# A loop over 24 attention tiles, written out as a straight program, in a decoder layer with two attentions and a mixture of experts

## What is computed

```python
def layer(x, ctx, mask):                     # x (16, 256, 256), ctx (16, 77, 256), f32
    x = layernorm(x + attn(x))               # causal self-attention, 16 heads of 64, then projection
    x = layernorm(x + xattn(x, ctx, mask))   # attention over 77 context rows, 16 heads of 16
    x = layernorm(x + moe(x))                # 8 experts, top 2, capacity 1280, a fallback FFN, gelu
    return x
```

## Time and profile before

| | |
|---|---|
| median of 3 runs | 1939.02 us (1936.5 to 1940.05) |
| the profiled execution | 1935.39 us, its span 1933.6 us |
| granted clock of TensorE, mean over the span | 0.927 of full |
| TensorE busy | 1597.7 us, 21,330 matmuls |
| VectorE, ScalarE, GpSimd busy | 1258.6, 1036.6, 707.3 us |
| moved by DMA | 162.80 MB in 136,447 packets |

### The profile page before, as it was taken

The page is one execution under the profiler, slowest core; times in us unless marked ns, Lnnn a source line. Parts: engine busy times, 40 slices in busy tenths (PEclk is TensorE's granted clock), DMA queues, the critical chain, the costliest instruction groups (busy, mean ns, idle before and its releaser), DMA issues. The chain is left out here.

```text
span 1933.6 us, 59530 instructions
## 1 busy us (share of the span) xinstructions
PE 1597.7 (83%) x21330; PEld 1388.0 (72%) x21330; DVE 1258.6 (65%) x3008; ACT 1036.6 (54%) x2581; POOL 707.3 (37%) x910
## 2 busy tenths in 40 slices
PE   1999989898898988989889899985169999999920
PEld 1788878787787877878778788874068888888810
DVE  4577767676676766767667677764675555555556
ACT  4566666666666666666566666552004444444424
POOL 1134345453344534435343353342003334333311
PEclk9999999999999999999999999996559999999965
DMA  5342222223222232222233221100731111111145
GB/s 151 106 131 95 69 88 75 72 67 103 85 76 75 67 98 85 82 75 67 69 103 93 69 73 55 55 19 6 314 119 41 49 51 46 47 49 50 45 154 196
DMA packets 136447, 162.80 MB, mean 84 GB/s; under 512 B 78334, under 2 KB 110206, under 8 KB 133760
## 3 DMA queue, kind: packets, MB, share of 16 engines
q1 hardware_dynamic: 125056, 136.94, 21.5%
q0 software_dynamic: 6912, 17.84, 3.0%
q10 hardware_dynamic: 4224, 4.19, 0.6%
HBM read 93.92 MB, written 66.06 MB: 83 GB/s over the span
## 5 line engine op out<-in xcount | busy, mean ns | idle before, releaser
L1311 PE MATMUL ps_e<-xt,wres 128*128 128x128 f16 x3456 | 359.4, 220 | 0.2
L1311 PEld LDWEIGHTS ps_e<-xt,wres 128*128 x3456 | 292.1, 98 | 73.2 <-issue 0.6
L1360 ACT ACTIVATE act_g<-ps_e,b 128x128 f32<-128x128 f32 x576 | 164.3, 368 | 227.0 <-PE ps_e L1311 116.5
L1318 PE MATMUL ps_e<-wres,g_hi 128*128 x576 | 217.5, 379 | 1.1 <-DVE g_lo L1390 1.1
L881 POOL TENSOR_TENSOR o_st<-o_norm,o_st 128x256 f16<-128x256 f32 x128 | 85.9, 671 | 338.0 <-ACT o_st L602 337.9
L386 PE MATMUL ps<-x_hi,w_q 128*128 128x128 f16 x2048 | 197.2, 222 | 0.0
L590 ACT ACTIVATE probs<-ps,nbias 128x128 f32<-128x128 f32 (+1 forms) x512 | 187.3, 417 | 8.4
L386 PE MATMUL ps<-x_hi,w_k 128*128 128x128 f16 x2048 | 187.2, 219 | 0.0
L386 PE MATMUL ps<-x_lo,w_q 128*128 128x128 f16 x1024 | 181.9, 222 | 1.2 <-issue 1.2
L707 DVE TENSOR_REDUCE nmax<-ps 128x1 f32<-128x128 f32 (+1 forms) x512 | 157.5, 349 | 38.2 <-PE ps L401 34.3
L386 PE MATMUL ps<-x_lo,w_k 128*128 128x128 f16 x1024 | 176.5, 219 | 0.0
(11 more groups left out here) (257 smaller groups left out, 4830.2 us busy)
## 6 DMA issues: line engine op xcount, KB each, us to landing
piece<-in_moe_w SPq DMA_DIRECT2D x24, 768.0 KB, 6.5
w_scr<-piece_pair SPq DMA_DIRECT2D x24, 768.0 KB, 5.1
wres<-w_scr SPq DMA_DIRECT2D x18, 1024.0 KB, 22.3
v_scr<-v_tok SPq DMA_DIRECT2D x32, 512.0 KB, 2.7
v_pos<-v_scr SPq DMA_DIRECT2D x32, 512.0 KB, 4.5
z_scr<-zero SPq DMA_DIRECT2D x32, 256.0 KB, 3.7
f_z<-z_scr SPq DMA_DIRECT2D x8, 1024.0 KB, 5.7
x_t<-in_xT SPq DMA_DIRECT2D x32, 128.0 KB, 5.9
```

What stands on the lines that cost most here:

```text
L1311: last = mm(out, w(c * FF + f * P, b, P), xt[:, t % 2, a, c], start=(m == 0), stop=(m == 5))
L1318: mm(out[:, 0:2 * D], g_hi[:, t % G_BUFS, f], w(KC * FF + f * D, 0, 2 * D), start=(f == 0), stop=False, skip_group_check=True)
L1360: nc.scalar.activation(act_g[:, k % 2, f], ps[:, 3 + 2 * (k % 2) + f // 4, (f % 4) * P:(f % 4 + 1) * P], ACT.Gelu, bias=bias[:, f:f + 1], ...
```

## The change

The `Fori` of twelve turns with two steps each becomes a Python loop over 24 whole numbers, which writes every step out. `steps` no longer needs the engine. Nothing else is edited; with s a whole number the values of waits and the addresses are constants.

```diff
--- before.py
+++ after.py
@@ -258,7 +258,7 @@
 
     block = ctx.enter_context(nc.Block())
 
-    def steps(eng, step):
+    def steps(step):
 
 
         step(-1, 1, "NA")
@@ -266,9 +266,8 @@
         step(1, 1, "NABC")
         step(2, 0, "NABCD")
         step(3, 1, "NABCD")
-        with eng.Fori(2, BATCH - 2, 1) as b:
-            step(2 * b, 0, "NABCDW")
-            step(2 * b + 1, 1, "NABCDW")
+        for s in range(4, TILES - 4):
+            step(s, s % 2, "NABCDW")
         step(TILES - 4, 0, "NABCD")
         step(TILES - 3, 1, "NABCD")
         step(TILES - 2, 0, "ABCD")
@@ -353,7 +352,7 @@
                 sp.dma_start(weight_rows(io)[:, bass.ds(n * 2 * PIECE, 2 * PIECE)],
                              piece_pair[:].rearrange("p b k n -> p (b k n)")).then_inc(s_w_out, 16)
 
-        steps(sp, step)
+        steps(step)
         sp.wait_ge(s_z_out, 16 * (CODES // P) // 2)
         sp.wait_ge(s_w_out, 16 * (PIECES + 1))
         for p in range(2):
@@ -557,7 +556,7 @@
                 if "D" in stages and g >= 3:
                     stage_d(s - 2, p, g)
 
-        steps(pe, step)
+        steps(step)
 
 
     @block.scalar
@@ -676,7 +675,7 @@
                     act.wait_ge(s_w_hi, 2 * (s - 4) + 1)
                     nc.scalar.activation(piece[:], piece[:], ACT.Copy, scale=WP_UP).then_inc(s_w_hi, 1)
 
-        steps(act, step)
+        steps(step)
 
 
     @block.vector
@@ -851,7 +850,7 @@
         nc.vector.memset(v2_hi[:], 1.0).then_inc(s_one, 1)
         nc.vector.memset(sm[:], NEG2).then_inc(s_neg, 1)
         dve.wait_ge(s_neg, 1)
-        steps(dve, step)
+        steps(step)
 
 
     @block.gpsimd
@@ -952,7 +951,7 @@
                     nc.gpsimd.tensor_tensor(piece_pair[:, at, 1], piece[:].rearrange("p (b n) -> p b n", n=WBLOCK)[:, at], piece_pair[:, at, 0],
                                             ALU.subtract).then_inc(s_w_lo, 1)
 
-        steps(pool, step)
+        steps(step)
 
 
 def weight_rows(io):
```

## The result

The changed kernel takes 1874.74 us (1873.56 to 1876.16, four runs) against 1937.82 us before (four runs, the three of the table above and one more): ratio 0.9672, interval 0.9656 to 0.9687, 63.1 us or 3.3% faster. The profiled execution took 1876.16 us, its span is 1874.3 us against 1933.6.

A forecast was written before the change was run, and what follows sets the result against it. TensorE, 83% busy, was taken to bound the kernel, with idle gaps and a lower clock at each loop jump. 54.1 us for jumps plus 4.1 for registers, 58.2 off the 1939.02 median, gave 1880.8 us, range 1873 to 1890.

The forecast's parts named there:

- The jumps: Eleven jumps back of TensorE's loop: removing them was to save 54.1 us, idle time and slower matmuls together.
- Gaps: TensorE idle before L409, the body's first matmul, after each of eleven jumps: 35.7 us in all, to vanish.
- Lower clock: Even steps behind a jump run at 0.93 to 0.97 of full clock; 16.4 us to be saved.
- The register work: Sequencers computing wait values and addresses in the loop: 0 to 8.2 us to be saved, middle 4.1 taken.
- weight pieces: Extra ScalarE and GpSimd copies in the loop's steps, a possible other source of the 0.34 us a step.
- The instruction stream: Code fetch in the 24 steps: TensorE's packets from 130 to about 90, other engines' up 40 to 50; costed at nothing.
- Rival 1: Other engines' straight code arrives late, holding them about 3.25 us a packet: 2027 us, slower; chance 0.02.
- Rival 2: Weight pieces or x's load would end the loop's steps late anyway: at the limit no change, 1939; chance 0.02.
- next late thing: In straight steps, TensorE's waits before L493 and L526, about 3 us a step, were to remain the bound.
- Rival 3: Late TensorE packets or lower clock in the straight 24 steps, losing 1 us a step: 1905; chance 0.06.
- Rival 4: Python steps with whole numbers would emit other code than with a register; chance 0.01 at most.
- The sum: Whole kernel: 54.1 + 4.1 = 58.2 us saved, ends 54.1 and 62.3, giving 1880.8 us; chance 0.90.

The follow-up runs named there:

- the announced jump: The kernel before, loop and registers kept, with a hint on TensorE's loop announcing its jump back; 1884.81 us, ratio 0.9726.
- the shorter body: The kernel before with its loop, each projection taking only the first of its three products, TensorE's body 1,595 records instead of 2,139; 1869.26 us, with less work.
- the code sizes: The changed kernel plus a block behind its end: every engine loops over bodies of some 100 to 2,200 satisfied waits, in two runs; the block's time means nothing.
- the jump to held code: The changed kernel with, on TensorE alone, a two-turn loop of one semaphore increment behind each odd step, 12 jumps back; 1875.17 us.
- the registers' run: The changed kernel's 24 written-out steps, but each pair takes its tile number from a register, without a jump; 1883.39 us, ratio 0.9715.

## Why the prediction was right, and where it was off

**The jumps.** Predicted 54.1 us, from the two undisturbed loop steps of the earlier trace rows. The runs confirm both parts and the way they hang together. Gaps: 35.7 us gone. Cause: the fetch of a target that is not held (the announced jump, the shorter body, the code sizes, and against them the jump to held code). Lower clock: TensorE's busy time in the steps went from 868.65 to 844.15 us. Not all of these 24.5 us are time of the kernel. The fair comparison is the registers' run, which has the same register work and no jumps. There TensorE is busy 844.86 us, 23.8 less than in the loop before, and idle 72.5 us, where the loop before, without its gaps, has 66.8. TensorE, late behind each jump, thus waited 5.7 us less for others, 5.0 of it for VectorE's o_norm. 35.7 us of gaps and 23.8 of slower work less these 5.7 are the 53.8 by which the two differ. The prediction took the step lengths (16.4 us) and not the busy time (22.0), and so had this right without naming it; its sentence that the 16.4 shows as busy time leaves 5.6 us open. The loop without its jumps is 917.3 us as predicted (917.0 from 12 x (37.67 + 38.75)).

**The register work.** This is the term that was mis-sized. The prediction bounded it by 0 and 8.2 us, put it down to registers or weight pieces, and took the middle, 4.1. It measured 8.0 (917.32 - 909.28), and the weight pieces cost nothing. VectorE carries about 0.1 us a step and TensorE most of the rest. So the upper end was true. Both reasons that the prediction gave, that register work sits in the chains between engines and that the copies of the pieces fall into ScalarE's idle time, pointed there, and the middle was taken against them.

**The instruction stream.** About 90 packets were predicted for TensorE's 24 steps, 98 came; 40 to 50 for the others, 37 came in place of 4. None held an engine: the 24 step lengths agree to 0.02 us. Rival 1 is out, though its price was real. A fetch that is not ahead cost the other engines 2.4 to 3.3 us in the table above; straight code is brought ahead, a far jump is not.

**Rival 2** (the gap as a cover) is out as it was put, since L492 and L525 wait no longer than they did. In small there was a cover: the wait for o_norm, 5.7 us before and 12.0 after. The prediction's next late thing was mis-sized too: the waits before L493 and L526 are 1.6 us a step ((31.4 + 6.7) / 24), and the 3 us are all of TensorE's idle time in a step. **Rival 3** (late packets) did not occur in straight code; late packets did occur, in small, in the loop with the announced jump. **Rival 4** is out, since the order and count of matmuls are the same.

**The sum.** Predicted 58.2, with ends of 54.1 and 62.3. In the steps it is 61.9, of which 54 for jumps and 8 for registers; between the medians 63.1, with 1.2 us of scatter outside the steps in it. The measured 1874.74 lies 6.1 us under the 1880.8 forecast and near the low end of the range: 3.7 us by the steps, nearly all of it the register term, 1.2 by that scatter, and 1.2 because the fourth run of the kernel before took its median from 1939.02 to 1937.82, which is luck of the runs. The Trainium skill, "Advanced Engine Details and Errata", section Control Flow Timing, has 108 ns for a compare-and-branch. With the target held the records here show 45 to 56 ns on four engines and 208 ns on TensorE, about a factor of two on either side; with the target not held TensorE's took 3.6 to 4.3 us, so a sum by that figure would have missed the whole effect.

## What to carry to other kernels

In a profile, a first instruction of a loop body that waits for "issue", and a compare-and-branch of 4 us on TensorE, mean a body that TensorE can't hold; a body of up to 1,600 instructions, or straight code, is free of it. The price of such a jump was the gap of 3.2 us and 1.5 to 1.9 us more for the clock behind it, with a part of the delay hidden in waits for other engines. On the other engines look behind the branch, not at it: the limit is 300 to 320 instructions. And a step of the same kind outside the loop, in the same trace, is the best price list there is: here its length gave the two ends of the sum, 54.1 and 62.3 us, within 0.4 us of what was measured (53.8 and 61.9).

## What was not expected of the hardware

That the four other engines refetch a loop at 320 instructions, so near the 228 of VectorE's body here: a body of four tiles already passes it. That an announced jump on TensorE takes 0.46 us and leaves the second block late by 0.5 to 1.4 us. And that constants against registers are worth 0.33 us in a step of 38 with no instruction of any engine's visible work changed.
